# Attention on one core: sixteen of 36 probability tiles transposed on the way through memory, instead of seven

## What is computed

```python
x = x + attn(layernorm(x));  x = x + ffn(layernorm(x))
# attn:
q = rmsnorm(x @ Wq.T); k = rmsnorm(x @ Wk.T); v = x @ Wv.T
scores = einsum('bkgqd,bksd->bkgqs', q, k) / sqrt(128)
p   = softmax(scores + alibi_bias, causal)          # rows: queries, columns: keys
out = einsum('bkgqs,bksd->bkgqd', p, v)             # needs p with the keys on partitions
return out @ Wo.T
```

## Time and profile before

| | us |
|---|---|
| median of three runs (2137.99 to 2138.62) | 2138.23 |
| the profiled execution | 2138.16 |
| its span (first to last instruction) | 2136.3 |
| group 2, first batch (start of `scores.0.0` to the next group's) | 130.7 |
| group 10, second batch | 124.7 |

### The profile page before, as it was taken

How to read it: one execution, slowest core, us unless ns; L and a number is a source line. 1 busy time by engine, 2 the same in 40 slices (tenths; PEclk the granted TensorE clock), 3 DMA queues, 4 the chain that set the end, 5 groups by cost and what they waited for, 6 DMA issues and landing times.

```text
span 2136.3 us, 33509 instructions
## 1 busy us (share of the span) xinstructions
PE 2083.0 (98%) x11772; PEld 1786.4 (84%) x11772; DVE 1355.6 (63%) x3431; ACT 1148.2 (54%) x3314; POOL 936.1 (44%) x984
## 2 busy tenths in 40 slices
PE   7999999999999999999999999999999999999997
PEld 6888888888888888888888888888888888888885
DVE  6656656566565665658876556566566656656676
ACT  4555545555454654645445555555555555555552
POOL 3443434444444443444443544435453443545443
PEclk9999999999999999999999999999999999999998
DMA  4152141511415125051350422313041231304112
GB/s 158 64 140 75 30 130 64 154 60 40 133 54 150 60 55 157 16 154 55 110 157 7 113 70 68 101 50 92 28 107 62 67 102 50 89 30 106 44 36 73
DMA packets 329095, 176.81 MB, mean 83 GB/s; under 512 B 243800, under 2 KB 301144, under 8 KB 320736
## 3 DMA queue, kind: packets, MB, share of 16 engines
q1 hardware_dynamic: 305264, 72.41, 15.3%
q10 hardware_dynamic: 23664, 102.25, 12.8%
HBM read 99.11 MB, written 75.50 MB: 82 GB/s over the span
## 4 chain that ended last, share of the span: by engine, by line
PE 83%; DVE 4%; issue 4%; DMA 3%; SPq 2%; POOL 2%; ACT 2%; ACTq 0%; DVEq 0%; POOLq 0%
PE s_ps L1026 17%; PE q_ps L1026 15%; PE y_ps L1026 15%; PE o_ps L1026 15%; PE turn_ps L1113 13%; PE turn_ps L1026 5%; DMA p_raw<-p_bounce 3%; SPq L568 2%; POOL probs_odd L799 1%; PE turn_ps L1107 1%; PE y_ps L1186 1%; DVE pT_lo L898 1%; DMA p_bounce<-probs_odd 1%; DVE y L955 0%; DVE oT_lo L949 0%
## 5 line engine op out<-in xcount | busy, mean ns | idle before, releaser
L799 POOL TENSOR_TENSOR probs_odd<-probs_odd,p_inv 128x256 f32<-128x256 f32 (+3 forms) x256 | 316.4, 1256 | 326.9 <-DVE p_inv L928 326.9
L706 ACT ACTIVATE pT_hi<-turn_ps 128x512 fp32r<-128x512 f32 x464 | 271.6, 597 | 316.2 <-PE turn_ps L1113 315.9
L799 POOL TENSOR_TENSOR probs_even<-probs_even,p_inv 128x128 f32<-128x128 f32 (+3 forms) x256 | 261.8, 1044 | 386.1 <-DVE p_inv L928 386.1
L898 DVE TENSOR_TENSOR pT_lo<-turn_ps,pT_hi 128x512 fp32r<-128x512 f32 x464 | 314.6, 684 | 146.2 <-ACT pT_hi L706 145.2
L921 DVE CUSTOM_DVE_ANT_0 probs_odd<-s_ps,rel 128x256 f32<-128x256 f32 (+3 forms) x256 | 209.3, 820 | 131.9 <-issue 131.4
L1026 PE MATMUL s_ps<-kT_hi,qT_hi 128*128 128x512 f32 (+3 forms) x768 | 278.7, 363 | 2.6 <-DVE kT_lo L900 1.8
L1026 PE MATMUL s_ps<-kT_hi,qT_lo 128*128 128x512 f32 (+3 forms) x768 | 262.9, 342 | 0.0
L1026 PE MATMUL s_ps<-kT_lo,qT_hi 128*128 128x512 f32 (+3 forms) x768 | 262.1, 341 | 0.0
L720 ACT ACTIVATE probs_odd<-probs_odd,neg_max 128x256 f32<-128x256 f32 (+3 forms) x256 | 211.9, 832 | 76.0 <-DVE neg_max L921 75.9
L921 DVE CUSTOM_DVE_ANT_0 probs_even<-s_ps,rel 128x128 f32<-128x128 f32 (+3 forms) x256 | 174.0, 686 | 118.0 <-issue 117.2
L1026 PE MATMUL o_ps<-pT_hi,v_hi 128*128 128x512 f32 x576 | 243.9, 423 | 1.9 <-DVE pT_lo L898 0.9
(11 more groups left out here) (110 smaller groups left out, 4578.6 us busy)
## 6 DMA issues: line engine op xcount, KB each, us to landing
p_raw<-p_bounce SPq DMA_DIRECT2D x448, 64.0 KB, 2.3
p_bounce<-probs_odd SPq DMA_DIRECT2D x64, 256.0 KB, 2.3
wq_kept<-wqT_hi ACTq DMA_DIRECT2D x8, 1024.0 KB, 5.8
wq_kept<-wqT_lo ACTq DMA_DIRECT2D x8, 1024.0 KB, 8.4
wo_kept<-woT_hi ACTq DMA_DIRECT2D x8, 1024.0 KB, 8.1
wo_kept<-woT_lo ACTq DMA_DIRECT2D x8, 1024.0 KB, 10.2
p_bounce<-probs_even SPq DMA_DIRECT2D x64, 128.0 KB, 1.8
wqT_hi<-wq_kept ACTq DMA_DIRECT2D x8, 1024.0 KB, 4.8
```

The costliest lines, as they stand in the source:

```text
L706: nc.scalar.activation(target, bank, ACT.Copy).then_inc(sems["high"], 1)
L799: nc.gpsimd.tensor_tensor(row, row, p_inv[:, s % 2, h:h + 1].to_broadcast((P, L)), ALU.mult).then_inc(sems["normalise"], 1)
L898: nc.vector.tensor_tensor(target, bank, upper.bitcast(F32), ALU.subtract).then_inc(sems["low"], 1)
```

## The change

`MEMORY_TILES` gets more entries, so that 1+2+2+3+3+5 = 16 tiles of a group go through memory:

```diff
-MEMORY_TILES = {5: (5,), 6: (5, 6), 7: (4, 5, 6, 7)}
+MEMORY_TILES = {2: (2,), 3: (2, 3), 4: (3, 4), 5: (3, 4, 5), 6: (4, 5, 6), 7: (3, 4, 5, 6, 7)}
```

`keep_wq` now writes the weights of its own group instead of those of the next, and stands early in the group:

```diff
             def keep_wq(w):
-                after(act, "low", "wq", w + 1, C - 1)
-                act.dma_start(wq_kept[w + 1, 0], wqT_hi[:].rearrange("p c n -> p (c n)").bitcast(F32)).then_inc(wq_spilled, 16)
-                act.dma_start(wq_kept[w + 1, 1], wqT_lo[:].rearrange("p c n -> p (c n)").bitcast(F32)).then_inc(wq_spilled, 16)
+                after(act, "low", "wq", w, C - 1)
+                act.dma_start(pieces(wq_kept, w, 0), wqT_hi[:].bitcast(F32)).then_inc(wq_spilled, 16)
+                act.dma_start(pieces(wq_kept, w, 1), wqT_lo[:].bitcast(F32)).then_inc(wq_spilled, 16)
```

The kept weights lie in HBM in pieces of 512 numbers (2 KB) instead of whole rows of 1024 or 2048 numbers, for all three kinds, written and read alike:

```diff
-        wkv_kept = nc.dram_tensor("wkv_kept", [NG, 2, P, C * 2 * HD], F32).ap()
-        wq_kept = nc.dram_tensor("wq_kept", [NG, 2, P, C * W512], F32).ap()
-        wo_kept = nc.dram_tensor("wo_kept", [NG, 2, P, G * DM], F32).ap()
+        wkv_kept = nc.dram_tensor("wkv_kept", [NG, 2, C // 2, P, W512], F32).ap()
+        wq_kept = nc.dram_tensor("wq_kept", [NG, 2, C, P, W512], F32).ap()
+        wo_kept = nc.dram_tensor("wo_kept", [NG, 2, G, P, DM], F32).ap()
+
+        def pieces(kept, g, part):
+            return kept[g, part].rearrange("c p n -> p c n")
+
+        def pairs(turned):
+            return turned[:].rearrange("p (a c) n -> p a (c n)", c=2).bitcast(F32)
```

More of the change, by code:

```diff
@@ L630, in keep_wkv @@
                 after(act, "low", "wkv", w + 1, 1)
-                act.dma_start(wkv_kept[w + 1, 0], wkvT_hi[:].rearrange("p c n -> p (c n)").bitcast(F32)).then_inc(wkv_spilled, 16)
-                act.dma_start(wkv_kept[w + 1, 1], wkvT_lo[:].rearrange("p c n -> p (c n)").bitcast(F32)).then_inc(wkv_spilled, 16)
+                act.dma_start(pieces(wkv_kept, w + 1, 0), pairs(wkvT_hi)).then_inc(wkv_spilled, 16)
+                act.dma_start(pieces(wkv_kept, w + 1, 1), pairs(wkvT_lo)).then_inc(wkv_spilled, 16)
             def keep_wq(w):
-                after(act, "low", "wq", w + 1, C - 1)
-                act.dma_start(wq_kept[w + 1, 0], wqT_hi[:].rearrange("p c n -> p (c n)").bitcast(F32)).then_inc(wq_spilled, 16)
-                act.dma_start(wq_kept[w + 1, 1], wqT_lo[:].rearrange("p c n -> p (c n)").bitcast(F32)).then_inc(wq_spilled, 16)
+                after(act, "low", "wq", w, C - 1)
+                act.dma_start(pieces(wq_kept, w, 0), wqT_hi[:].bitcast(F32)).then_inc(wq_spilled, 16)
+                act.dma_start(pieces(wq_kept, w, 1), wqT_lo[:].bitcast(F32)).then_inc(wq_spilled, 16)
             def keep_wo(w):
                 after(act, "low", "wo", w, G - 1)
-                act.dma_start(wo_kept[w, 0], woT_hi[:].rearrange("p c n -> p (c n)").bitcast(F32)).then_inc(wo_spilled, 16)
-                act.dma_start(wo_kept[w, 1], woT_lo[:].rearrange("p c n -> p (c n)").bitcast(F32)).then_inc(wo_spilled, 16)
+                act.dma_start(pieces(wo_kept, w, 0), woT_hi[:].bitcast(F32)).then_inc(wo_spilled, 16)
+                act.dma_start(pieces(wo_kept, w, 1), woT_lo[:].bitcast(F32)).then_inc(wo_spilled, 16)
             def back_wkv(w):
@@ L647, in back_wkv @@
                 act.wait_ge(wkv_spilled, 32 * NG)
-                act.dma_start(wkvT_hi[:].rearrange("p c n -> p (c n)").bitcast(F32), wkv_kept[g, 0]).then_inc(wkv_back, 16)
-                act.dma_start(wkvT_lo[:].rearrange("p c n -> p (c n)").bitcast(F32), wkv_kept[g, 1]).then_inc(wkv_back, 16)
+                act.dma_start(pairs(wkvT_hi), pieces(wkv_kept, g, 0)).then_inc(wkv_back, 16)
+                act.dma_start(pairs(wkvT_lo), pieces(wkv_kept, g, 1)).then_inc(wkv_back, 16)
             def back_wq(w):
@@ L654, in back_wq @@
                 act.wait_ge(wq_spilled, 32 * NG)
-                act.dma_start(wqT_hi[:].rearrange("p c n -> p (c n)").bitcast(F32), wq_kept[g, 0]).then_inc(wq_back, 16)
-                act.dma_start(wqT_lo[:].rearrange("p c n -> p (c n)").bitcast(F32), wq_kept[g, 1]).then_inc(wq_back, 16)
+                act.dma_start(wqT_hi[:].bitcast(F32), pieces(wq_kept, g, 0)).then_inc(wq_back, 16)
+                act.dma_start(wqT_lo[:].bitcast(F32), pieces(wq_kept, g, 1)).then_inc(wq_back, 16)
             def back_wo(w):
@@ L661, in back_wo @@
                 act.wait_ge(wo_spilled, 32 * NG)
-                act.dma_start(woT_hi[:].rearrange("p c n -> p (c n)").bitcast(F32), wo_kept[g, 0]).then_inc(wo_back, 16)
-                act.dma_start(woT_lo[:].rearrange("p c n -> p (c n)").bitcast(F32), wo_kept[g, 1]).then_inc(wo_back, 16)
+                act.dma_start(woT_hi[:].bitcast(F32), pieces(wo_kept, g, 0)).then_inc(wo_back, 16)
+                act.dma_start(woT_lo[:].bitcast(F32), pieces(wo_kept, g, 1)).then_inc(wo_back, 16)
             def high(w, of, *which):
```

## The result

The changed kernel takes **2100.21 us** (median; 2099.21 to 2102.15), the kernel before 2138.43 us on the same chip. The ratio is 0.982, with a 95% interval of 0.980 to 0.984. The forecast was 2074 us with a range of 2052 to 2108: faster as foreseen, inside the range, 26 us above the forecast. The profiled execution has a span of 2100.4 us.

A forecast was written before the change was run, and what follows sets the result against it. The prediction took TensorE, busy 98% of the span, to bound the kernel. From 2138 us it took 63 for turns and 15 for relief, added 14 for new waits and 0 for the prologue: 2074 us, range 2052 to 2108.

The forecast's parts named there:

- What bounds the kernel: Whole span: TensorE, busy 98%, sets the pace nearly everywhere; work taken from it counts in full if operands arrive in time.
- Rival 3: TensorE was not the bound; turns only filled time waiting for `max`, `exp` and `normalise`: 2138 us, chance 2%.
- The turns, 63 us: On TensorE, 9 turns fewer in each of 16 groups, 144 at 0.44 us: 63 us less; lower end 52.
- The relief, 15 us with ends 0 and 23: Ends of first-batch groups: weight writes leave row block 7's fetches, reducing waits and half clock: 15 us back.
- The new waits, 14 us with ends 1 and 30: `values` waiting for `lower_p` in row blocks 2 to 7, for 144 more tiles through memory: +14 us.
- The sign that I had named for this term: New waits mis-sized if TensorE's waits for `pT_lo`, or `qn` and `y` behind waiting flips, sum far from 14 us.
- The start, 0 within 4: Prologue: order changes and query weights need not be written there, same bytes loaded: 0, within 4 us either way.
- The sum: Whole kernel: 2138 - 63 - 15 + 14 + 0 = 2074 us, a factor of 0.970.
- Rival 1: Transfers collide at new places, 4.5 us each; one in each of 16 groups gives 2147 us, slower; chance 7%.
- Rival 2: Each of 256 tiles makes TensorE wait 0.15 us, 38 us, behind held-up queues; relief eaten: 2113 us, chance 9%.
- Rival 4: No cost at all: new waits of 1 us and full relief, 2053 us; chance 8%.
- The signs I had named: L1134 less by 576, second-batch groups 121 to 122 us, `add_y` waits and half clock mostly gone, q1 near 34%, GpSimd 1124 us.

The follow-up runs named there:

- the turns alone: Kernel before, nothing moved to memory, nine tiles per group neither turned nor split (wrong in value): 2092.80 us, ratio 0.980.
- the moved write: Kernel before with only the queries' kept weights written back in the next group's third row block, all tiles as before: 2109.53 us, ratio 0.987.
- Half the write: Kernel before with only the upper half (1 MB of 2) of the queries' kept weights written back early: 2115.59 us, ratio 0.990.
- the larger pieces: Changed kernel with fetches in pieces of 512 bytes in place of 128 (wrong in value): 2099.02 us, ratio 0.982.
- the one ring: Changed kernel with the four places of `pT` shared, each tile taking the first free, not two each for turned and fetched: 2091.86 us, ratio 0.978.
- the old tables of the start and the three special groups: Changed kernel with the start and groups 7, 8 and last on the tables of before (7 tiles through memory): 2093.72 us, ratio 0.980.
- the edits of order: Four reorderings in the second batch (normalisation of queries, turn of k, two query products) against old tables plus one ring (2087.80 us): 2074.81 us.
- the kernel without the path through memory: Kernel before with the queries' weights written later and nine tiles per group neither turned nor split (wrong in value): 2056.79 us, ratio 0.962.
- The fastest version: Changed kernel with old tables in the start and groups 7, 8 and last, one ring of `pT` places and four edits of order: 2074.81 us, ratio 0.971.

## Why the prediction was right, and where it was off

- **What bounds the kernel.** Right. The span moved with TensorE's work, VectorE at 65% and GpSimd at 53% did not take over. The last group is the exception: there the turns gave little or nothing. **Rival 3**, that TensorE was not the bound, fell with it: the turns alone gave 43 to 44 us.
- **The turns, 63 us.** The price per turn was right (3.7 to 3.8 us per group of the second batch for 9, 0.41 to 0.42 each), the sum was 53 behind the moved write. The step that failed is to multiply by all 16 groups: by the starts of the groups with and without the turns, behind the moved write, the last group gives 1.6 us (without the moved write 0, a difference within what its clock does) and groups 0 to 6 give 3.1 each, where 9 x 0.44 are 4.0.
- **The relief, 15 us with ends 0 and 23.** Measured 28. I had worked out 23 in full and took less, because Wo's load and a fifth tile stay. Even the full 23 was short, and the run moves only one of the two writes. The cost of one collision was mis-sized: I took 16.6 / 7 = 2.4 us of wait, and the three groups without a half-clock stretch got back 2.7 to 2.9 each. Half the write already brings 22.
- **The new waits, 14 us with ends 1 and 30.** This is the term that was mis-sized most: measured, it is 43 us. The row that I scaled from, 0.21 us a tile with all collisions, is exceeded: 43 for 144 tiles are 0.30 each. I looked at the distance from fetch to flip, which is the transfer, and there is little to win at the transfer (the larger pieces: 39 us less waiting, 1 us of time). I didn't look at what the upper copy waits for behind the flip, although it stood in the rows: 27.4 us behind products with 112 tiles. With 256 tiles on two places it is 132.5. Of the 43 us the one ring gives 8 to 9 back, the old tables of the start and the three special groups 5 to 6 (4 on top of the ring), the edits of order 11 to 13, of which 2 to 4 are an old wait. That is about 25; the rest is not taken apart, nor are the 16 us in which TensorE is not idle. The sign that I had named for this term would not have shown it either: TensorE's waits for GpSimd's `pT_lo` and for `qn` sum to 8.1 + 7.2 = 15.3 us, as forecast, and before they were 0.6 + 6.9 already.
- **The start, 0 within 4.** 1.6 us more. TensorE's longest wait there is now 9.2 us for the load of Wq, where it was 8.6 for a VectorE item.
- **The sum.** 2138 - 53 - 28 + 43 = 2100. Three terms were off, by +10, -13 and +29, and two of them nearly cancelled; the forecast missed by the third. That the time lies inside the range is in part luck: with the turns and the new waits as measured and the relief at my 15 us, it would have been 2113, outside.
- **Rival 1** (transfers meet everywhere) fell: the DMA share is 0.46 to 0.51 by group, and the time doesn't change with the packets. Transfers do meet, in full stretches at other places (from 1515 to 1520 us the share is 1.08), but TensorE is busy for all of these 5 us. **Rival 2** had the size, and its 2113 us is nearer to the measured time than my 2074: 38 us of new waits, 0.15 us for each of 256 tiles, against 0.17 now. It put them down to late tiles behind queues, and its other half, that the relief is eaten, was wrong. **Rival 4** (no cost) fell; it describes the kernel without the path through memory, 2053 against 2057.
- **The signs I had named.** L1134 less by 576, q1 at 33.4% and GpSimd at 1113 us came as said, and so did the end of the `add_y` waits and of the half clock in groups 0 to 6; `flip_p` still waits up to 4.6 us for a transfer, but no `y` behind it. A group of the second batch was to be at 121 to 122 us and is at 123.3: this one sign pointed to the mis-sized term.
- **What stays open.** The fastest version is still 18 us above the 2056.8 without the path. Of these 9 are turns that it keeps in group 7, group 8 and the last (4.3, 3.3 and 1.6 us). The other 9 or so, mostly in the start and the first batch, where single groups differ by 1 to 3 us from version to version, have no run of their own; in groups 10 to 13 it is 0.7 us a group below that kernel, by its edits of order. Nor was it told apart what GpSimd's time costs by the chain and by the port.

## What to carry to other kernels

When more work is sent round the bounding engine, don't ask first whether the transfer is in time; ask for each buffer on the way who must be done before it can be filled again, since the wait for a place is already in the trace of before as a small row and grows with the count. Price a gain stage by stage: where a stage ends on another wait, as the last group here, less work on the busiest engine is worth little or nothing. And test a change of two parts by its parts: the smaller part, one moved write, gave 28 of the 38 us, and most of the tile path's 33 us came only after its waits were mended.

## What the hardware showed that I had not expected

VectorE's instructions became longer while GpSimd worked. In the changed kernel's last group, the two engines:

```profile
2071.89 2.49 POOL L826 TENSOR_TENSOR pT_lo<-p_raw,pT_hi 128x512 fp32r<-128x512 f32 x2 [7.06 <-ACT pT_hi L735]
...
2073.29 1.24 DVE L1020 TENSOR_TENSOR low_gated<-f_logits,f_gates 128x128 f32<-128x128 f32 x1
```

Without GpSimd's subtractions the same instruction of the program reads

```profile
2059.24 0.29 DVE L1022 TENSOR_TENSOR low_gated<-f_logits,f_gates 128x128 f32<-128x128 f32 x1
```

It takes 1.24 us in place of 0.29, and it ends at 2074.53, just after GpSimd's second subtraction (2074.38). The mean of these 16 instructions is 376 ns before, 646 in the change and 301 without the subtractions; that of the `kv_raw` scaling, which reads two operands too, goes from 1195 to 1399 and back to 1200. `pT_lo` of a turned tile, which reads one of its operands from PSUM, keeps its 684 ns. This agrees with the Trainium skill, SBUF — State Buffer, section SBUF: two separate sides. By it VectorE and GpSimd share one pair of ports; where a VectorE instruction has two inputs in SBUF and a GpSimd instruction reads SBUF, the one that starts second is blocked for the whole instruction of the other, not slowed in proportion. So GpSimd at 53% is not free cover: each of its subtractions can hold up a VectorE instruction that lies on the path, as here ahead of `turn.lora.6`, which waits 2.04 us where it waits 0.46 without the subtractions. It goes the other way too: at 429.26 us of the kernel before the `kv_raw` scaling starts first and keeps its 1.18 us, and the subtraction that starts 0.8 us behind it takes 1.51 us instead of 1.31 in the mean.
